# Four graph layers in one block: barriers between the layers taken out, each layer's first batch computed beside the last batch of the layer in front

## What is computed

```python
x = _layernorm(x + _L0_gnn_ref(x, L0_gnn_W, L0_gnn_a, adj))          # first: additive attention
x = _layernorm(x + _L1_gnn_ref(x, w0, b0, wa, ba, adj))              # second: one softmax per feature
x = _layernorm(x + _L2_gnn_ref(x, adj, L2_gnn_W, L2_gnn_a))          # third: additive attention
x = _layernorm(x + _L3_gnn_ref(x, adj, Wh, bh, Wo, bo, gamma, beta)) # fourth: dot-product, 4 heads, then one
# additive: Wh = x @ W; e = leaky_relu(Wh @ a1 [i] + Wh @ a2 [j]); elu(softmax(mask(e)) @ Wh)
# feature:  feat = softplus(...); softmax over the neighbours of feat * wa + ba, for each feature; weighted sum of feat
# dot:      h = x @ Wh.T per head; softmax(mask(h h.T)) @ h + b; leaky_relu; the same again after Wo; layer norm
```

## Time and profile before

| | |
|---|---|
| median of 3 runs | 2091.6 us (2090.79 to 2094.11) |
| profiled execution, its device time | 2092.67 us |
| profiled execution, its span | 2090.9 us |
| PE busy, share of the span | 91% |
| DVE busy | 78% |
| ACT busy | 60% |
| POOL busy | 28% |
| mean granted PE clock | 0.959 of full speed |

### The profile page before, as it was taken

The page is one execution under the profiler, slowest core; times in us unless marked ns, Lnnn a source line. Parts: engine busy times, 40 slices in busy tenths (PEclk is TensorE's granted clock), DMA queues, the critical chain, the costliest instruction groups (busy, mean ns, idle before and its releaser), DMA issues.

```text
span 2090.9 us, 51901 instructions
## 1 busy us (share of the span) xinstructions
PE 1913.1 (91%) x22356; PEld 1186.8 (57%) x22356; DVE 1626.3 (78%) x1913; ACT 1250.6 (60%) x2298; POOL 587.9 (28%) x453
## 2 busy tenths in 40 slices
PE   6999759995999659999999999999999999999983
PEld 4888637774888534455455455455455554554543
DVE  3999828874999657787887887888888888878863
ACT  3677756652777636655656656656656656656552
POOL 0233238872223300021221311212212212212214
PEclk8999969997999879999999999999999999999996
DMA  6000000000000000001101001000011010010010
GB/s 162 3 4 3 3 1 1 1 1 2 4 3 3 2 5 20 24 12 37 27 12 37 21 17 37 22 17 27 13 36 27 12 37 27 12 37 27 12 38 20
DMA packets 50348, 42.20 MB, mean 20 GB/s; under 512 B 33096, under 2 KB 36744, under 8 KB 50120
## 3 DMA queue, kind: packets, MB, share of 16 engines
q1 hardware_dynamic: 50120, 38.89, 6.8%
HBM read 25.76 MB, written 4.72 MB: 15 GB/s over the span
## 4 chain that ended last, share of the span: by engine, by line
PE 57%; DVE 5%; POOL 1%; issue 1%; ACT 0%; DMA 0%; SPq 0%; ACTq 0%; POOLq 0%; DVEq 0%
PE fourth_ps_out L1378 21%; PE fourth_ps_scores L1330 7%; PE fourth_ps_out L1392 6%; PE fourth_ps_scores L1333 5%; PE fourth_ps_scores L1336 5%; DVE fourth_weights L1034 3%; PE fourth_ps_scores L1354 2%; PE fourth_ps_prep L1295 2%; PE fourth_ps_prep L1305 2%; PE fourth_ps_scores L1363 1%; PE fourth_ps_scores L1357 1%; PE fourth_ps_scores L1360 1%; PE fourth_ps_prep L1287 1%; PE fourth_ps_prep L1265 1%; DVE fourth_cat L1013 1%
## 5 line engine op out<-in xcount | busy, mean ns | idle before, releaser
L1034 DVE TENSOR_TENSOR fourth_weights<-fourth_weights,keep_mask 128x1024 f32<-128x1024 f32 x512 | 666.5, 1342 | 109.2 <-ACT fourth_weights L1183 107.2
L1183 ACT ACTIVATE fourth_weights<-fourth_ps_scores 128x1024 f32<-128x1024 f32 x512 | 497.3, 1024 | 357.9 <-PE fourth_ps_scores L1336 337.2
L1378 PE MATMUL fourth_ps_out<-fourth_weights,fourth_x_stage 128*64 128x512 f32 x2048 | 498.0, 605 | 4.4 <-DVE fourth_weights L1034 4.4
L1378 PEld LDWEIGHTS fourth_ps_out<-fourth_weights,fourth_x_stage 128*64 128x64 f32 x2048 | 124.3, 136 | 250.4 <-issue 217.1
L1330 PE MATMUL fourth_ps_scores<-fourth_g_high,fourth_x_high 64*128 64x512 f32 x1024 | 230.1, 446 | 2.6 <-DVE fourth_g_low L1001 2.4
L1330 PEld LDWEIGHTS fourth_ps_scores<-fourth_g_high,fourth_x_high 64*128 64x128 f32 x1024 | 96.2, 184 | 201.3 <-issue 101.4
L1333 PE MATMUL fourth_ps_scores<-fourth_g_high,fourth_x_low 64*128 64x512 f32 x1024 | 202.7, 392 | 0.0
L1336 PE MATMUL fourth_ps_scores<-fourth_g_low,fourth_x_high 64*128 64x512 f32 x1024 | 201.6, 390 | 0.0
L1190 ACT ACTIVATE fourth_weights<-fourth_ps_scores 128x1024 f32<-128x1024 f32 x128 | 125.2, 1026 | 113.3 <-PE fourth_ps_scores L1363 113.3
L1041 DVE TENSOR_TENSOR fourth_weights<-fourth_weights,keep_mask 128x1024 f32<-128x1024 f32 x128 | 153.1, 1237 | 43.3 <-ACT fourth_weights L1190 43.3
L434 DVE SCALAR_TENSOR_TENSOR first_weights<-first_ps_row,first_gain,keep_mask 128x1024 f32<-128x1024 f32 x128 | 159.3, 1267 | 2.5 <-ACT first_ps_row L535 2.5
(11 more groups left out here) (264 smaller groups left out, 3010.1 us busy)
## 6 DMA issues: line engine op xcount, KB each, us to landing
fourth_recip_wide<-recip_out SPq DMA_DIRECT2D x128, 128.0 KB, 3.0
setup_adj<-in_adj SPq DMA_DIRECT2D x8, 512.0 KB, 6.8
fourth_h_high<-fourth_h_high SPq DMA_DIRECT2D x32, 128.0 KB, 2.9
fourth_h_low<-fourth_h_low SPq DMA_DIRECT2D x32, 128.0 KB, 2.5
out<-keep_x SPq DMA_DIRECT2D x16, 256.0 KB, 2.6
dens_out<-fourth_mixture SPq DMA_DIRECT2D x64, 4.0 KB
keep_x<-in_x SPq DMA_DIRECT2D x1, 512.0 KB, 11.1
fourth_dens<-dens_out SPq DMA_DIRECT2D x32, 8.0 KB, 1.6
```

Source lines behind the costliest of these rows:

```text
L1034: dve.tensor_tensor(buf, buf, keep.mask[:, st.t, cols(half)].bitcast(F32).unsqueeze(1) .to_broadcast([P, 2, HALF]), ALU.mult).then_inc(wei ...
L1183: act.activation(weights[st.slot + half][:, :], ps_scores[half][:, :], ACT.Exp)\
L1378: last = pe.matmul(ps_out[rows(g), cols(half)], x_stage[st.s][:, st.t, g, :], weights[st.slot + half][:, cols(g)], start=(st.t == 0), stop ...
```

## The change

All five parts now issue into one block, and semaphores are cleared once, at the end of the program. `Memory` no longer has a release. The three layer functions became stages: they return their operations as functions, and three new classes (`FirstToSecond`, `InSecond`, `ThirdToFourth`) say at which step of a running layer an operation of the next layer, or a finishing step of the one in front, is issued. Tiles and banks are laid out so that the layers that overlap do not clash where work of both is under way.

- All weights are loaded in the opening: those of the first layer and `x` of batches 0 and 1 by ACT, the rest by SP behind `adj`. `x` of batches 2 to 5 comes ahead of the later weights and 6 to 15 behind them.
- The opening projects batch 0 of the first layer between the transposes of `adj`. The last tile of the mask is copied by DVE. `find_empty` stands behind the first `weigh`.
- The preparation of the third layer's and the fourth layer's weights (`preparation`) is spread over steps 0 to 7 of the second layer.
- The last two batches of the first layer carry the second layer's steps for batches 0 and 1. Step 15 of the second layer carries the projections for the third. The last two batches of the third layer carry the fourth layer's staging of batch 0.
- The finishing steps of a layer's last batches (the `*_late` functions) are issued between the first steps of the next layer.
- The second layer's steps run from 0 to 15 (POOL to 16).
- `keep.x` loses its 17th batch of zeros, `values` is 65 wide where it was 128, and some pairs of semaphores have become one that counts by two.

The core of the diff:

```diff
-        if self.semaphores:
-            self.nc.clear_and_free_semaphores(self.semaphores)
-            self.nc.all_engine_barrier()
...
+    def scalar():
+        load_additive(act, 0, "L0_gnn_W", "L0_gnn_a")
+        act.dma_start(keep.x[:, 0:2, :, :], x_rows(ins)[:, 0:2, :, :]).then_inc(keep.first_x_loaded, 16)
+        for i in range(TILES - 1):
...
+            if i == 3:
+                additive.copy_x(0)
+            if i == 5:
+                additive.copy_hidden(0)
+                additive.copy_mean(0)
+        additive.factors(0, 0)
+        additive.copy_x(1)
...
+    def vector():
+        for t in range(TILES):
+            dve.wait_ge(loaded[t], 16)
+            dve.tensor_scalar(rows[:, t, :], adj[:, t, :], 0.0, None, ALU.is_gt).then_inc(masked, 1)
+            if t == 0:
+                weights.copy_w(0, first_w)
+            if t == 2:
+                weights.copy_products(0, first_products)
+            if t == 5:
+                additive.find_tile_top(0)
+            if t == 6:
+                additive.find_minus_top(0)
+                additive.find_top(0)
+        additive.copy_tops(0)
+        dve.wait_ge(turned_full, TILES)
...
+class FirstToSecond:
...
+        if b == BATCH - 1:
+            if at == 2:
+                feature.find_tile_top(0, 0)
+            if at == 3:
+                feature.find_top(0)
+            if at == 6:
+                feature.lower_totals(0, 0)
+                feature.shift(0, 0)
+            if at == 7:
+                feature.split(0, 0)
...
+class InSecond:
...
+        if k == 0:
+            if at == 2:
+                additive.scalar_late(0, 0)
+                additive.scalar_late(0, 1)
+        if (k, at) == (2, 2):
+            additive.scalar_late(0, 2)
+        if (k, at) == (3, 2):
+            additive.scalar_late(0, 3)
...
+class ThirdToFourth:
...
+        if b == BATCH - 1:
+            if at == 2:
+                dot.lower_x(0, 0)
+            if at == 4:
+                dot.multiply_g(0, 0, 0)
+            if at == 7:
+                dot.lower_g(0, 0)
...
+        if b == BATCH - 1:
+            if at == 0:
+                dot.round_x(0, 0)
+            if at == 2:
+                dot.round_g(0, 0)
...
+        if b == BATCH - 1:
+            if t == 0:
+                dot.turn_x(0, 0)
+            if t == 3:
+                dot.make_g(0, 0, 0)
+            if t == 5:
+                dot.norm_g(0, 0)
...
+            @block.vector
+            def _(dve):
+                start.vector()
+                additive.vector(0, beside_first)
+                feature.vector(beside_second)
+                additive.vector(BATCH, beside_third)
+                beside_third.vector_turn()
+                dot.vector(beside_third)
```

3281 lines of the change are left out of this document (1823 added, 1458 removed).

## The result

The changed kernel takes 2029.24 us (median of 4 runs, 2027.78 to 2031.62) against 2092.12 us of the kernel before, measured beside it: a ratio of 0.970, 95% interval 0.9683 to 0.9717. That is 63 us won where 96 were forecast, and 2029 lies above the range of 1979 to 2014. The profiled execution spans 2025.5 us (2090.9 before), so 65.4 us of span are to be placed.

The account below looks back on a forecast made before the run. Chains of waits at the opening and three layer changes, 142.7 us, were the most to win. Terms -13 - 33 + 6 - 22 - 37 + 2.5 = -96.5 us gave span 1994.4, time 1995; range 1979 to 2014.

Parts of the forecast that it names:

- Opening: Up to batch 0's fourth weight tile: 13 us gained, 20 if DVE's waits cost nothing, 9 if PE runs at half clock.
- The rule on issuing engines: Opening: engines' transfers share 16 transfer engines, so ACT's x load gains no bandwidth and delays adj; own path 1.3 us better.
- First to second: Up to the second layer's first attention matmul: tail, barrier, loads and empty steps go; gain 33 us, between 30 and 35.
- the lengthening of the last batch: First layer's last batch: added DVE work and the wait at find_top(0) make the last multiply end 4.2 us later.
- Inside the second layer: Late first-layer work and weight preparation cost 6 us; 2 if DVE's waits absorb them, 12 if POOL stretches DVE's operations.
- rival (a): Crowding: every upper cost holds, DVE and POOL collide where late work overlaps; 72 us gained, 2020 us; chance 0.20.
- Second to third: Up to the third layer's fourth weight tile: gain 22 us after projection, an 11 us chain and late norm; ends 18, 27.
- Third to fourth: Up to the fourth layer's first multiply: gain 36.8 us; 39 if the ELU wait is hidden, 33 if masks are held.
- Fourth layer: Late ACT blocks in the fourth layer cost 2.5 us, ends 0 and 6; batches stay at 80.65 us.
- rival (c): Fourth layer slowed through DVE's masks by its new place in memory and banks; about 2131 us; chance 0.03.
- (d): Overlap fails because a late semaphore wait serializes; only barriers and loads go, some 12 us at four places; 2044; chance 0.05.
- Rival (b): Queues kinder than followed: opening and both additive waits hidden, 115 us gained; 1977 us; chance 0.12.

Follow-up runs that it names:

- e3_x_front: Changed kernel with the first load of x issued by SP behind the second piece of adj, not by ACT; 2022.9 us.
- e4_open_apart: Changed kernel with the projection of batch 0 behind the mask on PE, DVE and ACT, loads left as they are; 2014.4 us.
- e9_x_pieces: e7_all with the first x load issued as in e3_x_front and the last x load cut into five pieces, each behind a further first-layer batch; 1996.9 us.
- e10_write_top: e9_x_pieces with the first layer's last ACT write at step 6 of the second layer and find_top(0) behind the fifth weight tile; 1993.1 us.
- e5_pool_late: Changed kernel with the first layer's last inverse deviation on POOL, and the ACT write needing it, moved from step 3 to step 4; 2023.4 us.
- e6_prep_parcels: Changed kernel with the later weights' preparation cut into parcels behind shift on DVE, in steps 4 to 13 of the second layer; 2021.5 us.
- e11_parcels_end: e6_prep_parcels with the parcels back at the end of DVE's step and PE's parts one step later; 2028.9 us.
- e7_all: Changed kernel with e4_open_apart, e5_pool_late and e6_prep_parcels together, late DVE work of steps 1 to 3 behind shift, round_x later; 1999.0 us.
- e1_prep_apart: Changed kernel with PE's preparation parts in the second layer one step behind the DVE parts they need; 2024.7 us.
- e2_prep_later: Changed kernel with the whole weight preparation six steps later in the second layer; 2028.3 us.

## Why the prediction was wrong, point by point

**Opening, forecast -13, measured +3.4.** The step that failed is "`x` for batches 0 and 1 is one such piece in size and now travels among them, so the last comes about 1.3 us later". I priced what the load of `x` takes from `adj` and not what `adj`, and SP's next load of `x` (1 MB, issued at 5.98), take from it: it took 18.5 us, not one slot of 1.4. Issued from SP it took 6.8 (`e3_x_front`), so its place counts and not its size. By 16 us ACT's queue had moved 0.25 of its 0.56 MB, in packets of 256 bytes, and SP's 4.4 MB, mostly in packets of 4 KB. Whether `x` also stood behind the four small loads that ACT issues ahead of it, no run separates. Nor does `x` travel at the rate of `adj`: 217 GB/s from 16 to 20 us, with hardly anything but `x` under way, and 395 from 8 to 12. So the chain that I followed to 19.4 at `find_tile_top` reached it at 32.2, 12.8 us late, part of that too at the lower clock (0.50 from 24 to 28 us). The same step left out the columns of `a`, which came at 9.48, with DVE idle 4.26 us in front of mask row 1. The rest of the 16.4 is mostly the clock: the count at 6.24 and the row matmuls near 2, which I had at 4.00 and 1.10. The prediction's lower bound of 9 allowed for a slow clock in the count alone. `e3_x_front` gives back 10.6 of it by the transfer and `e4_open_apart` 14.6 by the order. Both together give 16.6 and not the sum of 25, so they are two ways into the same chain. The rule on issuing engines that I weighed there was right, and I applied it in one direction only.

**First to second, -33 against -29.5.** The mechanism was right. `find_top(0)` waited 1.46 us (about 1.6 foretold), and the chain from `shift` to the end of `split` took 5.0 us (261.75 to 266.76; 4.68 in the earlier trace rows). The term that was mis-sized is the lengthening of the last batch, 4.2 us forecast. The last multiply ended 264.8 against 254.17 before, 3.4 of that inherited from the opening, so 7.2. Two waits were not in my sum: 1.17 us at `find_tile_top` for POOL's product and 1.15 at `shift` for `spread_top`. In `e9_x_pieces`, and with `find_top` moved in `e10_write_top`, these are the rows (DVE, `shift` of each):

```profile
247.16 0.69 DVE L1839 TENSOR_TENSOR second_shifted<-second_product,second_ps_wide 128x512 f32<-128x512 f32 x1 [1.14 <-PE second_ps_wide L2036]
```

```profile
244.60 0.69 DVE L1839 TENSOR_TENSOR second_shifted<-second_product,second_ps_wide 128x512 f32<-128x512 f32 x1
```

**Inside the second layer, +6 against +20.2.** Here the working failed in kind. "In step 0 DVE and POOL have room" and "its waits of 1.49 take it up" treat late work as a quantity that slack absorbs. Of the 14.2 us missed, 5.4 are one wait that the change added and I never named: POOL's `inverse_deviation` behind DVE's variance of the same step, with POOL's whole step and, through ACT, PE behind it (`e5_pool_late`). I had listed "5 us to POOL" and not asked which engine is ahead in this loop. Another 7.0 are the preparation at the end of DVE's step, where it came back when it was moved (`e6_prep_parcels`), and `e11_parcels_end` puts 6.6 of these down to the place, PE's wait of 2.2 for a parcel of the same step included. Its work on DVE was put at 6 to 8 us, measured 9.9 in the changed kernel and 6.6 behind `shift`. The largest price in that sum, 2.39 for four `wh_twice`, was not too small: POOL had a copy of 1.99 us beside it in that row (from 740.73), and behind `shift` the four take 0.82. What was missing is what a step costs when such a lump stands at a point of DVE's order without slack. The wait of 1.49 us does not take them up, for it stands at another point of the step. Some 2 us are an error of bookkeeping: the third layer's projection in step 15, which I had put under the next event (from the start of step 14 on, the stretch is 22.9 us instead of 20.7). What is left of the 20.2 is 5.6 us. That this is near my 6 is luck: 4.6 of it stand in steps 0 to 2 (13.5, 12.3 and 12.4 us in `e6_prep_parcels`, 11.9, 10.9 and 10.9 before), of which I had said that step 0 has room and the preparation is what costs. The rival (a), crowding, had this mechanism, with the right witness, but was capped at 12 us for this step and given 0.20. At 2020 it too lay 9 us below what was measured.

**Second to third, -22 against -24.2.** Held; moved by those 2 us it is -22.0. The chain of 11 us that I worked out took 13.7 (465.24 to 478.90) and the projection cost PE 2.2 us instead of 3.1.

**Third to fourth, -37 against -36.8.** Held, in its parts too: `apply_elu` waits 2.69 us for `round_x` (2.7 foretold) and the scores follow the last multiply at full clock. What was "hidden" there, `e7_all` could take: 4.3 us over that stretch.

**Fourth layer, +2.5 against +1.5; batches unchanged at 80.65.** Held, so rival (c), the slower fourth layer, is out. So is (d): every overlap took place. Rival (b), kinder queues, lies 52 us below what was measured. (Its sum takes 3 and 1 us for the second and the fourth layer, where the terms above it allow 2 and 0; that would make it 1975 and changes nothing.)

The sum: 16.4 + 3.5 + 14.2 - 2.2 + 0.2 - 1.0 = 31.1 us, which is 2025.5 - 1994.4. The range was too narrow. Its upper end, 2014, did not even let every cost reach its bound, which was rival (a) at 2020, and the bounds themselves assumed that nothing would stand in line: a transfer took one slot, and work laid into a loop took slack. Nothing in it stood for a wait that was not on my list.

## What to carry to other kernels

When work of one stage is laid into another's loop, first write down which engine runs ahead in that loop: a small operation on the leading engine that needs a same-step result of a following one costs the distance between the two (4.2 us of wait and 5.4 of step here), not its own length. Put extra work on an engine where it waits anyway, look at what its port neighbour does there, and keep the engine that needs the result a step behind: the same copies cost nothing that showed in DVE's wait and 6.6 us at the end of its step. And price a transfer that shares the queues by what all the others take from it, not only by what it takes from them; keep it off the in-order path of the chain that everything else waits for.

## What the runs showed of the hardware

- A short VectorE operation in the on-chip memory can take five times its length beside a GpSimd one: two `wh_twice` of 64 columns 2.03 us against 0.41, `w_aug` 0.76 to 1.03 against 0.19. Their ends coincide with the ends of the GpSimd operations, which were on 512 columns. Beside a GpSimd operation of 1.65 us on 8 columns the same instructions took 0.41 and 0.19 (`e6_prep_parcels`). A copy out of PSUM (`w_turned`) took 0.34 in either place.
- A transfer of 512 KB issued from ScalarE beside 4 MB of `adj` and 1 MB of `x` from SyncE took 18.5 us. Issued from SyncE behind the second piece of `adj` it took 6.8 (`e3_x_front`). One 512 KB piece of `adj` reached VectorE 1.40 us behind the one before.
- Eight matmuls behind 2.00 us of idle time took 3.41 us instead of 2.09 (`e1_prep_apart`), and in the 17.0 us step of the changed kernel the mean granted clock is 0.80. It is not a fixed price of a stall: behind 1.99 us of idle time in `e2_prep_later` and 2.15 in `e5_pool_late` the same eight took 2.08, and behind 1.56 in `e7_all` they took 3.03. What decides it these runs do not show.
- TensorE stood 1.9 to 2.8 us without a semaphore to wait for near 42 us, when a transfer of 2.6 MB was coming to its end, in three kernels with a dense opening, and in none once the transfer was in pieces. It stopped behind the same instruction each time and started again 1.3 to 1.4 us after a 16 KB packet of the queue "q8 instruction" had ended.
